# Ten embedding tables on one core: the long tables before the short ones

## The reference

```
embs    = [x @ w for x, w in zip(xs, ws)]
emb_sum = sum(embs)
q_emb   = sum((x ** 2) @ (w ** 2) for x, w in zip(xs, ws))
fm_ans  = 0.5 * (emb_sum ** 2 - q_emb)
out     = concatenate([fm_ans] + embs, axis=-1)
```

## Time and profile before

| what | value |
|---|---|
| median of 3 runs | 293.42 us (293.13 to 293.93) |
| the profiled execution, its own time | 295.52 us |
| its span in the profile | 293.8 us |
| DVE / ACT / PE busy | 240.9 / 228.4 / 224.0 us |
| moved by DMA | 113.18 MB, mean 385 GB/s |
| granted TensorE clock, mean | 0.965 of full speed |

### The profile page before, as it was taken

How to read it: one execution, slowest core, us unless ns; L and a number is a source line. 1 busy time by engine, 2 the same in 40 slices (tenths; PEclk the granted TensorE clock), 3 DMA queues, 4 the chain that set the end, 5 groups by cost and what they waited for, 6 DMA issues and landing times.

```text
span 293.8 us, 2917 instructions
## 1 busy us (share of the span) xinstructions
PE 224.0 (76%) x878; PEld 158.9 (54%) x878; DVE 240.9 (82%) x236; ACT 228.4 (78%) x271; POOL 88.2 (30%) x68
## 2 busy tenths in 40 slices
PE   0759988987987878784877877887877878787680
PEld 0548766755755555453554554555554555455470
DVE  3745999999899898867898888888888899868743
ACT  2399999987897787767978877887788787767731
POOL 1353243344304403116224224314404413121000
PEclk9968999998899999999999999999999999997977
DMA  7999999999999999999999999999999999999922
GB/s 214 413 401 422 385 391 416 423 352 400 418 417 423 415 419 420 421 334 381 419 414 421 416 423 420 419 418 420 421 415 424 417 416 422 418 338 387 336 105 76
DMA packets 21427, 113.18 MB, mean 385 GB/s; under 512 B 2656, under 2 KB 3808, under 8 KB 9760
## 3 DMA queue, kind: packets, MB, share of 16 engines
q1 hardware_dynamic: 16800, 106.18, 90.3%
q10 hardware_dynamic: 4608, 6.79, 6.5%
HBM read 110.07 MB, written 2.88 MB: 384 GB/s over the span
## 4 chain that ended last, share of the span: by engine, by line
DMA 67%; issue 18%; DVE 6%; ACT 5%; PE 2%; DVEq 0%; ACTq 0%; SPq 0%
DMA x_ring<-in_x_dram 63%; DVE is_one L433 5%; DMA whole<-in_w_dram 4%; ACT is_set L270 3%; PE sums L359 2%; ACT turned L281 1%; PE sums L366 1%; DVE total L470 0%; ACT L263 0%; ACT whole L263 0%; ACT results L286 0%; DVE results L473 0%; DVE results L476 0%; ACT turned L311 0%; DVE total L445 0%
## 5 line engine op out<-in xcount | busy, mean ns | idle before, releaser
L433 DVE TENSOR_SCALAR_CACHE_REDUCE is_one<-x_ring 128x2048 uint8<-128x2048 f32 (+3 forms) x108 | 226.7, 2117 | 36.4 <-DMA x_ring<-in_x_dram 36.3
L270 ACT ACTIVATE is_set<-x_ring 128x2048 fp32r<-128x2048 uint32 (+3 forms) x108 | 192.2, 1782 | 44.5 <-DMA x_ring<-in_x_dram 44.4
L359 PE MATMUL sums<-is_set,low 128*128 128x512 f32 x398 | 137.9, 429 | 61.9 <-ACT is_set L270 45.2
L359 PE MATMUL sums<-is_set,high 128*128 128x512 f32 x398 | 128.2, 404 | 0.0
L359 PEld LDWEIGHTS sums<-is_set,low 128*128 128x128 f32 x398 | 70.5, 196 | 106.4 <-ACT is_set L270 57.4
L359 PEld LDWEIGHTS sums<-is_set,high 128*128 128x128 f32 x398 | 77.7, 195 | 18.4
L338 POOL CAST high<-whole 128x1024 fp32r<-128x1024 f32 (+5 forms) x31 | 27.0, 872 | 173.8 <-ACT whole L263 173.8
L340 POOL TENSOR_TENSOR low<-whole,high 128x1024 fp32r<-128x1024 f32 (+5 forms) x31 | 60.6, 1955 | 2.5
L263 ACT ACTIVATE whole<-whole 128x512 f32<-128x512 f32 (+5 forms) x31 | 16.6, 538 | 5.0 <-DMA whole<-in_w_dram 5.0
L270 ACT ACTIVATION_READ_ACCUMULATOR is_set<-x_ring 128x1 f32 (+2 forms) x108 | 20.4, 189 | 0.0
L366 PE MATMUL sums<-identity,turned 128*128 128x128 f32 x80 | 12.1, 302 | 0.8 <-ACT turned L311 0.8
(11 more groups left out here) (17 smaller groups left out, 3.7 us busy)
## 6 DMA issues: line engine op xcount, KB each, us to landing
x_ring<-in_x_dram SPq DMA_DIRECT2D x91, 1024.0 KB, 18.8
x_ring<-in_x_dram SPq DMA_DIRECT2D x10, 512.0 KB, 13.1
whole<-in_w_dram ACTq DMA_DIRECT2D x20, 256.0 KB, 7.3
out_dram<-results SPq DMA_DIRECT2D x10, 256.0 KB, 13.1
x_ring<-in_x_dram SPq DMA_DIRECT2D x4, 448.0 KB, 12.5
x_ring<-in_x_dram SPq DMA_DIRECT2D x2, 320.0 KB, 9.0
whole<-in_w_dram ACTq DMA_DIRECT2D x3, 192.0 KB, 7.4
x_ring<-in_x_dram SPq DMA_DIRECT2D x1, 384.0 KB, 18.5
```

The lines of the kernel that those rows point to most:

```text
L270: nc.scalar.activation(is_set[chunk.k % SETS][0:chunk.rows, 0:chunk.n * BATCH], x_of(chunk).bitcast(U32), ACT.Sign, accum_out=set_counts[0 ...
L359: last = nc.tensor.matmul(sums[:, summing(n, half), :], w, x[0:chunk.rows, at:at + HALF], start=first, stop=False, skip_group_check=True)
L433: nc.vector.tensor_scalar(is_one[chunk.k % 2][0:chunk.rows, 0:chunk.n * BATCH], x_of(chunk), 1.0, None, ALU.is_equal, ALU.add, accum_out=o ...
```

## The change

Only the list `ORDER` changes: which tables come first. Chunk sizes, groups, ring, buffers and the last table stay. The rest of the program is derived from the list.

```diff
 ORDER = [
-    (8, [[1, 1]]),
+    (0, [FULL] * 12 + [[1, 1]]),
+    (1, [FULL] * 6 + [[1]]),
+    (2, [FULL, [2, 2, 2], [2, 2, 1, 1]]),
+    (3, [[2, 2, 2], [2, 1, 1]]),
+    (7, [[2, 1, 1]]),
     (9, [[1]]),
     (5, [[1, 1]]),
+    (8, [[1, 1]]),
     (4, [[2, 2, 1]]),
-    (7, [[2, 1, 1]]),
-    (3, [[2, 2, 2], [2, 1, 1]]),
-    (2, [FULL, [2, 2, 2], [2, 2, 1, 1]]),
-    (1, [FULL] * 6 + [[1]]),
-    (0, [FULL] * 12 + [[1, 1]]),
     (6, [[2, 2, 2, 1, 1]]),
 ]
```

## The result

The kernel with the new order takes 302.88 us in the median (302.22 to 303.65), before it took 293.68 us: ratio 1.031, 95% interval 1.028 to 1.033. It is 9.2 us slower. The forecast was slower by 1.7 us, with a range up to 298.4.

A forecast was written before the change was run, and what follows sets the result against it. DMA's x stream was taken to bound the kernel, its end hanging on chunk 105, ACT and PE. ACT's wait for table 8's weights delays DVE's last add: 293.42 + 1.7 = 295.1 us, range 292.8 to 298.4.

The forecast's parts named there:

- Direction: Whole kernel: slower, chance 0.70; same 0.22, faster 0.08; predicted time 295.1 us.
- ACT's and DVE's part of the mechanism: Near the end: ACT waits 1.7 us for table 8's weights, delaying DVE's adds; the last add comes 1.6 us later.
- the sum: Last 13 chunks, pitches added up: ACT starts chunk 105 at 279.0, PE's path gives the add 287.6, DVE's 287.9.
- With tails, 0.9 for 9 and 8: x stream of the last 13 chunks: tails cost 0.9 us for 9 and 8, 2.1 for table 6's; 25.8 us altogether.
- the stream of x should end at the same time: End of x loads: bytes and loads unchanged, so the stream still lands by 278.6 us.
- the backward sum: Landings reckoned back from 278.6 by 25.8 us: chunk 94 at 252.8, 93 at 251.5, 92 at 250.3.
- rival B: ACT near the end waits longer for weights, or twice: 297.6 us, with low clock 298.6; chance 0.16.
- The base: Starting time for the added 1.7 us: profiled span 293.8, own time 295.52, median of runs 293.42.
- The rule of the Trainium skill: DMA engines alternate queues by packets; weights among one-tile chunks then land in 4.7 us, and the order changes nothing.
- Rivals C and D: C: weights land in 5 us or less, 293.4, chance 0.22. D: high clock, tails hidden in ACT's backlog, 292.0, chance 0.08.
- D's high clock: PE at the end keeps the high clock: 7.1 us from chunk 105 to the copy, before 8.55.

The follow-up runs named there:

- the paired runs: Tails of tables 3, 8 and 9 loaded as 128 rows, in the new order and in the order of before: 297.03 us and 292.32 us.
- the third order: `ORDER` 0, 1, 8, 9, 5, 4, 7, 3, 2, 6, against the kernel before: 296.48 us with short tails, 288.24 us with full tails.

## Why the prediction was wrong, point by point

- **Direction, and ACT's and DVE's part of the mechanism, were right.** ACT stands still for table 8's weights after chunk 95; the next load goes out early and costs ACT 0.5 us at most; behind the standstill ACT needs 20.8 us to chunk 105 by the sum, 21.6 measured (262.19 to 283.78); PE then takes 7.1 by the sum, 6.98 measured, at the high clock; DVE sets the last add, 0.3 us after PE in the sum. From the first delayed add to the last one DVE needed 27.8 us, forecast 27.0. The experiments agree: moving the loads gives 1.8 us back once tails are full, moving the squares 2.5 with short ones.
- **The step that failed is the transfer cost of the short tables near the end: "With tails, 0.9 for 9 and 8".** I took a dip measured at the start of the kernel, and left the dearer tails of tables 2 and 3 out. In the profile after, 9 and 8 lose 2.0 us each and 3 loses 1.9; by the paired runs the three cost 6.7 us late and 2.2 early. The earlier trace rows had the better price, 2.1 us for table 1's tail in mid-kernel. With this falls "the stream of x should end at the same time", from which I reckoned every landing backwards: chunk 105 landed at 280.0, not 276.3. Dearer tails put into the backward sum alone would even have moved chunk 93 the wrong way, to an earlier landing. It landed at 253.36, not 251.5 (1.9 us), and the weights for table 8 took 8.8 us, not 6.7 (2.1 us). With 0.8 us on ACT, chunk 105 started 4.8 us late against the forecast, and the last add came at 292.73, 4.8 us after the 287.9 of the sum. I had named the longer landing as rival B, but with 1.5 us for it, and had not joined it with the late chunk; both go with the short tails.
- **The base.** The sum was made against a profiled execution that was itself 1.8 us above the median, and its excess was carried as if it belonged to every run. It hid 1.8 of the 2.5 us by which the medians differ more than the profiles.
- **The account of 9.2 us.** Order with clean transfers 5.0 us (waits for weights 1.8, the rest of the work at the tables' ends 3.2), short tails costing more where they now stand 4.0 to 4.5 us. That the 3.2 us are ACT's copies and DVE's adds is argued: ACT works nearly without a gap and takes chunk 105 3.3 us after its landing, DVE adds without a wait, and the third order pays part of it back. No run took these copies away.
- **The rule of the Trainium skill.** It gave 4.7 us, as an estimate, for weights among one-tile chunks. This case doesn't bear it out. In five profiles of this order with the tails of 9 and 8 short the load took 8.1 to 9.0 us, in four with them full 5.7 to 7.1. The shortest is still 1 us above the estimate, and the four differ by 1.4 us for a reason that no run shows.
- **Rivals C and D** didn't happen. D's high clock did, and was worth what was said; DVE and ACT came far too late for it.
- **Open.** Why a transfer of 80 or 112 rows over 16 engines slows everything in flight, and why its dip lasts 3 to 4 us in the first 67 us of the kernel and 5 to 6 later. Row shares of 8, a shallower ring and earlier short tails were tried and are not the answer, and being apart isn't either: side by side at 198 us, 8 and 9 still cost about 3.2 us. There they stood right behind another short tail; the two alone in mid-kernel weren't tried.

## What to carry to other kernels

What is late at the start of a kernel is paid back by any long stretch that waits for data; the same work in its last 30 us isn't. Where an order is changed, walk the last ring's worth of loads chunk by chunk, and take no price of a transfer from another place of the kernel without a bound several times as wide. And read dips in GB/s at full DMA share as a thing to remove, not as given: here 0.8 MB of zeros, which make every transfer 128 rows, save 7.4 us in the best of the three orders and 11.6 in the worst.

## What the runs showed of the hardware

- Loads of 80, 96 or 112 rows by 4 KB in a stream of 128-row loads slow the stream at full DMA share: 237 to 281 GB/s for 5 to 6 us against 419, about 2 us each. In the first 40 us of the kernel one such load, or two side by side, cost 0.9 us. Loading 128 rows instead (0.79 MB more in 104 MB) took 7.4 us off 293.7, and 11.6 off 302.9.
- Tails of which only 10, 12 or 14 engines take a share, 8 rows each (from the count of packets), are worse: 305.3 against 293.7 us.
- ACT's queue issued a weight load well before the engine came to it once nothing in between was awaited (262.54, with the chunk in front of it starting at 264.83).
- A weight load of 64 KB at the same place in the program took 8.1 to 9.0 us with the tails of 9 and 8 short, and 5.7 to 7.1 with them full.
